# Moving the normalisation step (subtract the mean, multiply by the reciprocal root) from DVE to POOL in a two-block transformer kernel

## The chip, the cores and the metric

The kernel runs on one core of one Trainium2 chip. The metric is the device time of one execution in microseconds (us). PE is the matrix engine, DVE the vector engine, ACT the scalar engine, POOL the GpSimd engine, SP the engine that only issues DMAs here.

## The reference, cut to what matters

Two blocks run over 16 sequences of 128 tokens with 128 channels and 16 heads of 8 channels. The first is a cross attention with a conditioned layer norm on both inputs; the second is a self attention, a cross attention and an MLP.

```python
def _ada_ln(x, c, W_ss, b_ss):                 # block 0, on x and on the context
    mu = mean(x); var = mean((x - mu) ** 2)
    h = (x - mu) / sqrt(var + EPS)
    scale, bias = split(silu(c) @ W_ss + b_ss, 2)
    return (1 + scale)[:, None, :] * h + bias[:, None, :]
x = x + attention(q(ada_ln(x)), kv(ada_ln(ctx))) @ Wp + bp
...
x = x + gate_a * (self_attention(modulate(_ln(x))) @ W_proj + b_proj)      # block 1
x = x + cross_attention(_ln(x), _ln(ctx)) @ W_cproj + b_cproj
x = x + gate_m * (gelu(modulate(_ln(x)) @ W_mlp1 + b_mlp1) @ W_mlp2 + b_mlp2)
```

Each `(x - mu) * rsqrt(var + eps)` is what the change is about.

## The kernel before, in words

**Work.** There are three attention layers (CROSS0, SELF1, CROSS1), then the MLP. A unit is one sequence in one layer: 48 units, in 12 groups of 4; the MLP has 4 more groups. Every engine runs its own program, written out by hand in a loop over ticks, from -10 to 53, and semaphores tie them together. In tick t the stages of several units stand side by side: scores of unit t+2, row maxima of t+2 and t+1, the second score product (with the row maximum folded in, "keyed") of unit t, the product with the values of t and t-1, and the output projection of t-2. There is a front of work once per group, spread over the ticks 4g-10 to 4g-7: the norm of x in the first (n = 0), the norm of the context in the second (n = 1, only where the layer has one), the projections to q, k, v in the rest. So there are 24 norms: 16 of x and 8 of the context.

**A norm.** DVE makes the statistics of four sequences (`norm_stats`: L705, L708, and L710, which adds epsilon). POOL makes the reciprocal root of 128x4 values by a power (`inverse_root`, L858). DVE then subtracts the mean and multiplies by the root, four instructions of 128x128 (`normalise`, L721), at the end of its tick. PE transposes the four results one tick later in program order (`transpose_normed`, L339), ACT scales and shifts them (`modulate`, L558 or L553), PE projects them (L349, L357). In CROSS1 the context's statistics are those of CROSS0, so DVE only adds another epsilon.

**The row maximum.** PE makes the scores of a unit in two halves (`scores`, L374), and each half waits until DVE has reduced the half before (`row_max`, L740, 1.2 us). After the second half POOL splits the 128x16 maxima into two bf16 parts (`split_max`, L865 and L867), PE turns them (`turn_max`, L382), DVE copies them out of PSUM (`copy_max_rows`, L749), SP sends them by DMA into rows of `stack_q`, and then PE may start the keyed scores of that unit (`keyed_scores`, L398).

**PSUM slots.** All small products of PE share three slots of `misc_ps` in a fixed order (`MISC_ORDER`). PE may take a slot when the use three places earlier has been read out. In a tick of CROSS0 with a norm, the slot of `transpose_normed` is that of the gate product before (read by DVE in `copy_gates`, L779), and the slot of `turn_summed` (L428) is that of `turn_max` (read by `copy_max_rows`).

**Orders around the change.** The order of DVE in a tick is

```python
row_max(tick + 2, 0); copy_max_rows(tick + 1); norm_stats(*norm); leave_rest(g3, 1)
add_branch(tick - 2); divide(tick - 1); row_max(tick + 2, 1)
normalise(*norm); copy_gates(tick); leave_rest(g2, 0)
```

and that of POOL is

```python
add_gated(tick - 3)  or  add_out_bias(tick - 2)
inverse_root(*norm); split_rest(g3, 1); split_max(tick + 2); split_rest(g2, 0)
```

(each where its unit or group exists; there is a norm in the first tick of a group's front, and in the second where the layer has a context norm). PE's order in a tick is keyed scores, first half (L398); scores of t+2, first half (L374); attend t-1 (L418); `turn_max` (L382); `transpose_normed` (L339); `project_out` (L440); keyed scores, second half; `turn_summed` (L428); scores, second half; projections; attend t; `turn_attn` (L433). `divide` (L755, L759) needs L428, and its result is turned by L433.

The other names: `x_bias` (L893) is x plus the output's bias, made by POOL for `add_branch` (L773); in SELF1 POOL makes the gated addition instead (L899, L901); `split_rest` (L877, L879) splits q and k into bf16 parts, on the two ticks of a group's front that have no norm in steady running.

## Time and profile before

| What | Value |
|---|---|
| Median of 3 runs | 353.94 us (353.48 to 354.7) |
| The profiled execution's own time | 353.89 us |
| Its span in the trace | 352.1 us |
| PE busy (matmuls) | 280.2 us, 80% |
| DVE busy | 248.9 us, 71% |
| ACT busy | 206.0 us, 59% |
| POOL busy | 130.4 us, 37% |
| Chain that ended last | PE 44%, DVE 25%, issue 15%, DMA 5%, ACT 4%, POOL 3% |
| of it the line of `normalise` (L721) | 6% |

The chain that ended last is followed back from the last instruction, at each step to what released it. "Issue" in it is time in which an engine waited for nothing that the profile shows. Engines are not busy in sum: at every point one of them holds the others up, and which one has to be read in the timeline.

### The profile page before, as it was taken

The numbers are of one execution on the slowest core, as the hardware profiler recorded it, in microseconds if no ns is written. First come the engines' busy times: TensorE is split into PE (matmuls) and PEld (weight loads), VectorE is DVE, ScalarE is ACT, GpSimd is POOL, SyncE is SP. The second block draws the span as 40 slices with busy tenths as digits, with TensorE's granted clock in tenths as the row PEclk, the third lists the DMA queues.
The fourth block names the chain that finished last, engine by engine and source line by source line (L and its number), as shares of the span: only waits on it lengthen the run. The fifth ranks groups of instructions, "written<-read, shape, count | busy, mean of one in ns | idle before, by whom it ended". The sixth has DMA issues, their size and how long they took to land.

```text
span 352.1 us, 10184 instructions
## 1 busy us (share of the span) xinstructions
PE 280.2 (80%) x3827; PEld 179.9 (51%) x3827; DVE 248.9 (71%) x630; ACT 206.0 (59%) x323; POOL 130.4 (37%) x252
## 2 busy tenths in 40 slices
PE   0415346988989899898988979889798878879894
PEld 0403224655656566565565656656565555544442
DVE  7374478798787877878788797887978787713104
ACT  1004224777675676767766757667667757775540
POOL 1863362522524315252453644536443131301000
PEclk9999685999999999999999999999999999999999
DMA  8901431323123222332322323322322300000013
GB/s 230 271 0 45 135 89 48 86 56 90 53 76 80 77 72 71 85 81 68 93 73 71 93 60 83 93 63 78 90 67 78 93 6 4 4 1 2 1 30 89
DMA packets 31904, 25.39 MB, mean 72 GB/s; under 512 B 4552, under 2 KB 31600, under 8 KB 31856
## 3 DMA queue, kind: packets, MB, share of 16 engines
q1 hardware_dynamic: 30624, 23.74, 25.1%
q10 hardware_dynamic: 1232, 1.00, 1.0%
q8 instruction: 31, 0.51, 0.6%
q14 instruction: 17, 0.14, 0.1%
HBM read 4.41 MB, written 1.05 MB: 16 GB/s over the span
## 4 chain that ended last, share of the span: by engine, by line
PE 44%; DVE 25%; issue 15%; DMA 5%; ACT 4%; POOL 3%; SPq 2%; ACTq 1%; DVEq 0%; POOLq 0%
PE misc_ps L349 7%; PE attn_ps L418 7%; DVE normed L721 6%; DVE neg_max L740 4%; PE keyed_ps L398 4%; DMA stack_q<-max_rows 4%; PE score_ps L465 4%; PE keyed_ps L454 4%; PE score_ps L374 3%; DVE stats L705 3%; PE misc_ps L428 3%; PE misc_ps L357 3%; DVE rest L732 2%; PE misc_ps L333 2%; ACT parts L572 2%
## 5 line engine op out<-in xcount | busy, mean ns | idle before, releaser
L740 DVE TENSOR_REDUCE neg_max<-score_ps 128x8 f32<-128x1024 f32 x96 | 116.7, 1216 | 15.0 <-PE score_ps L374 15.0
L592 ACT ACTIVATE probs<-keyed_ps 128x1024 f32<-128x1024 f32 x96 | 98.3, 1024 | 12.9 <-PE keyed_ps L398 10.4
L418 PE MATMUL attn_ps<-probs,values 128*32 128x128 f32 x1536 | 61.8, 279 | 0.4 <-ACT probs L592 0.4
L398 PE MATMUL keyed_ps<-stack_q,stack_k 64*128 64x128 bf16 x768 | 38.6, 221 | 10.9 <-DMA stack_q<-max_rows 9.8
L418 PEld LDWEIGHTS attn_ps<-probs,values 128*32 128x32 f32 x1536 | 36.1, 109 | 19.1 <-issue 10.6
L374 PE MATMUL score_ps<-stack_k,stack_q 62*128 62x128 bf16 x768 | 38.8, 221 | 8.9 <-DVE neg_max L740 8.9
L858 POOL TENSOR_TENSOR rstd<-var_eps,minus_half 128x4 f32<-128x4 f32 x24 | 24.4, 1016 | 57.7 <-DVE var_eps L710 57.7
L865 POOL CAST max_parts<-neg_max 128x16 bf16<-128x16 f32 x48 | 10.2, 212 | 89.9 <-DVE neg_max L740 89.7
L558 ACT ACTIVATE normed_t<-misc_ps,mod 128x128 f32<-128x128 f32 x48 | 18.0, 456 | 40.5 <-PE misc_ps L339 40.5
L339 PE MATMUL misc_ps<-ident,normed 128*128 128x128 f32 x96 | 18.3, 322 | 24.9 <-DVE normed L721 22.0
L609 ACT ACTIVATE attn_t<-misc_ps,bcol 128x128 f32<-128x128 f32 x48 | 17.6, 368 | 32.3 <-PE misc_ps L433 30.8
L398 PEld LDWEIGHTS keyed_ps<-stack_q,stack_k 64*128 64x128 bf16 x768 | 21.9, 95 | 25.1 <-DMA stack_q<-max_rows 15.4
L732 DVE SCALAR_TENSOR_TENSOR rest<-misc_ps,bcol_p,parts 128x512 f32<-128x512 f32 x24 | 18.0, 751 | 23.0 <-ACT parts L572 23.0
L374 PEld LDWEIGHTS score_ps<-stack_k,stack_q 62*128 62x128 bf16 x768 | 23.7, 96 | 19.3 <-DVE neg_max L740 11.6
L428 PE MATMUL misc_ps<-ident,summed 128*128 128x128 f32 x192 | 31.1, 284 | 2.7 <-ACT summed L600 0.3
L600 ACT ACTIVATE summed<-attn_ps 128x512 f32<-128x512 f32 x48 | 28.5, 593 | 3.6 <-PE attn_ps L418 3.6
L879 POOL TENSOR_TENSOR parts<-rest,parts 128x512 bf16<-128x512 f32 x24 | 27.7, 1155 | 1.9
L349 PE MATMUL misc_ps<-normed_t,w_qk 128*128 128x512 f32 x48 | 28.2, 676 | 0.0
L339 PEld LDWEIGHTS misc_ps<-ident,normed 128*128 128x128 f32 x96 | 11.9, 159 | 29.8 <-DVE normed L721 29.7
L572 ACT ACTIVATE parts<-misc_ps,bcol_p 128x512 bf16<-128x512 f32 x24 | 16.5, 687 | 15.6 <-PE misc_ps L349 15.6
L428 PEld LDWEIGHTS misc_ps<-ident,summed 128*128 128x128 f32 x192 | 20.1, 140 | 9.9 <-ACT summed L600 4.5
L877 POOL CAST parts<-rest 128x512 bf16<-128x512 f32 x24 | 14.6, 609 | 25.9 <-DVE rest L732 25.9
(92 smaller groups left out, 411.7 us busy)
## 6 DMA issues: line engine op xcount, KB each, us to landing
stack_q<-parts SPq DMA_DIRECT2D x72, 128.0 KB, 2.4
stack_k<-parts SPq DMA_DIRECT2D x72, 128.0 KB, 2.4
stack_q<-max_rows SPq DMA_DIRECT2D x96, 4.0 KB
xs<-in_x_dram SPq DMA_DIRECT2D x4, 256.0 KB, 4.4
cs<-in_ctx_dram SPq DMA_DIRECT2D x4, 256.0 KB, 5.1
out_dram<-xs SPq DMA_DIRECT2D x4, 256.0 KB, 2.3
w<-in_L_xcond_W_mlp_dram SPq DMA_DIRECT2D x2, 256.0 KB, 5.8
wmod<-in_L_xcond_W_mod_dram ACTq DMA_DIRECT2D x1, 384.0 KB, 5.7
```

The lines of the kernel that those rows point to most:

```text
L339: mm = pe.transpose(ps[:, j * T:(j + 1) * T], normed[:, n, j, :], ident[:, :])
L349: pe.matmul(take_misc("qk"[n], g), w_qk[:, s, n, :], normed_t[:, src, :, :], start=True, stop=True).then_inc(qk_ps, 1)
L374: mm = pe.matmul(score_ps[:, e, a * T:(a + 1) * T], stack_q[rows, g % STACKS, CP * c + a, cols], stack_k[rows, g % STACKS, CP * c + a, col ...
L398: mm = pe.matmul(keyed_ps[:, e, a * T:(a + 1) * T], stack_k[rows, g % STACKS, CP * c + a, cols], stack_q[rows, g % STACKS, CP * c + a, col ...
L418: mm = pe.matmul(attn_ps[at:at + QUAD, slot * T:(slot + 1) * T], values[:, u // PER % STACKS, u % PER, h, :], probs[:, n % 3, (CP * e + a) ...
L428: mm = pe.transpose(ps[:, i * 128:(i + 1) * 128], summed[:, u % 2, i, :], ident[:, :])
L592: act.activation(probs[:, n % 3, :], keyed_ps[:, :, :].rearrange("t e n -> t (e n)"), ACT.Exp, scale=float(D) ** -0.5).then_inc(probs_read ...
L600: act.activation(summed[:, u % 2, :, :].rearrange("p s t -> p (s t)"), attn_ps[:, :], ACT.Copy).then_inc(summed_ready, 1)
L732: dve.scalar_tensor_tensor(out=rest[:, n, :], in0=misc("qk"[n], g), scalar=bcol_p[:, r:r + 1], in1=parts[:, g % 2, n, 0, :], op0=ALU.add, ...
L740: dve.tensor_reduce(neg_max[:, u % 2, :, CP * c:CP * (c + 1)], score_ps[:, :, :].rearrange("t e (a k) -> t e a k", k=T), AX.X, ALU.max, ne ...
L858: pool.tensor_tensor(rstd[:, n, :], var_eps[:, n, :], minus_half[:, :], ALU.pow).then_inc(rstd_ready, 1)
L879: pool.tensor_tensor(parts[:, g % 2, n, 2, :], rest[:, n, :], parts[:, g % 2, n, 1, :], ALU.subtract).then_inc(split_ready, 1)
```

## The change

The function `normalise` moves from DVE's program to POOL's. Its four instructions stay the same (tensor_scalar with subtract and mult, mean and root read per partition), with the same two waits, and POOL runs them straight after its reciprocal root, ahead of `split_rest(g3, 1)` and `split_max(tick + 2)`. DVE's `norm_stats` gets a new wait: before it writes the statistics of input n, the last norm of that input must have been taken (`normed_ready`), since another engine now reads them. `norm_input` moves out to where both engines see it.

```diff
+        def earlier_norm(g, n):
+
+            return max((norms_to(*m) for m in NORMS[:norms_to(g, n) - 1] if m[1] == n), default=0)
...
@@ DVE, norm_stats
+                if earlier_norm(g, n):
+
+                    dve.wait_ge(normed_ready, earlier_norm(g, n))
...
@@ DVE
-            def normalise(g, n):
-                b0, b1 = batches(g)
-                src, mv = norm_input(g, n)
-                dve.wait_ge(rstd_ready, norms_to(g, n))
-                if g >= 1:
-
-                    dve.wait_ge(normed_ps, norms_to(g, n) - 1)
-                for j in range(PER):
-                    ins = dve.tensor_scalar(normed[:, n, j, :], src[:, b0 + j, :], mv[:, j, 0:1],
-                                            rstd[:, n, j:j + 1], ALU.subtract, ALU.mult)
-                ins.then_inc(normed_ready, 1)
...
@@ DVE, loop over ticks
                 if unit(tick + 2):
                     row_max(tick + 2, 1)
-                if norm:
-                    normalise(*norm)
                 if 0 <= tick < B:
                     copy_gates(tick)
...
@@ POOL
+            def normalise(g, n):
+                b0, b1 = batches(g)
+                src, mv = norm_input(g, n)
+                pool.wait_ge(rstd_ready, norms_to(g, n))
+                if g >= 1:
+
+                    pool.wait_ge(normed_ps, norms_to(g, n) - 1)
+                for j in range(PER):
+                    ins = pool.tensor_scalar(normed[:, n, j, :], src[:, b0 + j, :], mv[:, j, 0:1],
+                                             rstd[:, n, j:j + 1], ALU.subtract, ALU.mult)
+                ins.then_inc(normed_ready, 1)
...
@@ POOL, loop over ticks
                 if norm:
                     inverse_root(*norm)
+                    normalise(*norm)
                 if g3 is not None:
                     split_rest(g3, 1)
```

POOL's instructions in CROSS1, in the two ticks of a group that hold its norms of x and of the context. Before:

```order
L893 TENSOR_TENSOR x_bias<-xs,b_out 128x128
L858 TENSOR_TENSOR rstd<-var_eps,minus_half 128x4
L865 CAST max_parts<-neg_max 128x2x8
L867 TENSOR_TENSOR max_parts<-neg_max,max_parts 128x2x8
L893 TENSOR_TENSOR x_bias<-xs,b_out 128x128
L858 TENSOR_TENSOR rstd<-var_eps,minus_half 128x4
L865 CAST max_parts<-neg_max 128x2x8
L867 TENSOR_TENSOR max_parts<-neg_max,max_parts 128x2x8
```

With the change:

```order
L898 TENSOR_TENSOR x_bias<-xs,b_out 128x128
L851 TENSOR_TENSOR rstd<-var_eps,minus_half 128x4
L861 TENSOR_SCALAR normed<-xs,x_mv,rstd 128x128 x4
L870 CAST max_parts<-neg_max 128x2x8
L872 TENSOR_TENSOR max_parts<-neg_max,max_parts 128x2x8
L898 TENSOR_TENSOR x_bias<-xs,b_out 128x128
L851 TENSOR_TENSOR rstd<-var_eps,minus_half 128x4
L861 TENSOR_SCALAR normed<-cs,c_mv,rstd 128x128 x4
```

The four subtractions stand between the root and the split of the row maximum.

DVE's instructions in SELF1, from the norm of x of a group to the next tick (L770 is the branch of SELF1 in `add_branch`). Before:

```order
L710 TENSOR_SCALAR var_eps<-x_mv 128x4
L770 TENSOR_TENSOR branch<-misc_ps,b_out 128x128
L755 RECIPROCAL r_sum<-misc_ps 128x16
L759 TENSOR_TENSOR attn<-misc_ps,r_sum 128x128
L740 TENSOR_REDUCE neg_max<-score_ps 128x2x4
L721 TENSOR_SCALAR normed<-xs,x_mv,rstd 128x128 x4
L740 TENSOR_REDUCE neg_max<-score_ps 128x2x4
L749 COPY max_rows<-misc_ps 32x128
```

With the change:

```order
L717 TENSOR_SCALAR var_eps<-x_mv 128x4
L765 TENSOR_TENSOR branch<-misc_ps,b_out 128x128
L750 RECIPROCAL r_sum<-misc_ps 128x16
L754 TENSOR_TENSOR attn<-misc_ps,r_sum 128x128
L735 TENSOR_REDUCE neg_max<-score_ps 128x2x4 x2
L744 COPY max_rows<-misc_ps 32x128
```

The two reductions, one of the second half of a unit's scores and one of the first half of the next unit's, now follow each other.

## Rows read from the trace of the kernel before

**Rows 1.** The page: busy time of each engine, and PE's granted clock in 40 slices.

```profile
PE 280.2 (80%) x3827; PEld 179.9 (51%) x3827; DVE 248.9 (71%) x630; ACT 206.0 (59%) x323; POOL 130.4 (37%) x252
...
PEclk9999685999999999999999999999999999999999
```

**Rows 2.** Groups by line and form: busy us, mean ns | idle before, releaser.

```profile
L721 DVE TENSOR_SCALAR normed<-xs,x_mv,rstd 128x128 f32<-128x128 f32 x64 | 19.8, 372 | 4.8 <-POOL rstd L858 4.8
...
L721 DVE TENSOR_SCALAR normed<-cs,c_mv,rstd 128x128 f32<-128x128 f32 x32 | 9.6, 364 | 2.3 <-POOL rstd L858 2.3
```

**Rows 3.** Groups by line and form: POOL's other operations on 128x128.

```profile
L893 POOL TENSOR_TENSOR x_bias<-xs,b_out 128x128 f32<-128x128 f32 x32 | 15.1, 472 | 2.0 <-DVE xs L773 2.0
...
L841 POOL COPY w_qk<-wq 128x128 f32<-128x128 f32 x1 | 0.4, 389 | 0.0
...
L828 POOL TENSOR_SCALAR_AFFINE_SELECT ident<-ident 128x128 f32<-128x128 f32 x1 | 0.3, 293 | 0.2 <-POOL ident L826 0.2
L831 POOL CAST ident_b<-ident 128x128 bf16<-128x128 f32 x1 | 0.3, 291 | 0.1
```

**Rows 4.** Timeline, CROSS0, a tick with norm and gate, and POOL's next split: start us, us, instruction.

```profile
118.64 1.02 POOL L858 TENSOR_TENSOR rstd<-var_eps,minus_half 128x4 f32<-128x4 f32 x1 [3.11 <-DVE var_eps L710]
...
125.72 0.20 POOL L865 CAST max_parts<-neg_max 128x16 bf16<-128x16 f32 x1 [4.26 <-DVE neg_max L740]
125.99 0.22 POOL L867 TENSOR_TENSOR max_parts<-neg_max,max_parts 128x16 bf16<-128x16 f32 x1
...
120.29 1.25 DVE L721 TENSOR_SCALAR normed<-xs,x_mv,rstd 128x128 f32<-128x128 f32 x4
...
121.22 0.22 PE L382 MATMUL misc_ps<-ident_b,max_parts 128*32 128x128 bf16 x1
122.02 0.63 PE L339 MATMUL misc_ps<-ident,normed 128*128 128x128 f32 x4 [0.58 <-DVE gate L779]
```

**Rows 5.** Timeline, CROSS1, a tick with norm but no gate, and the next.

```profile
267.79 1.02 POOL L858 TENSOR_TENSOR rstd<-var_eps,minus_half 128x4 f32<-128x4 f32 x1 [2.67 <-DVE var_eps L710]
...
271.75 0.20 DVE L749 COPY max_rows<-misc_ps 32x128 bf16<-32x128 bf16 x1
...
273.27 1.21 DVE L740 TENSOR_REDUCE neg_max<-score_ps 128x8 f32<-128x1024 f32 x1
...
270.75 0.66 PE L339 MATMUL misc_ps<-ident,normed 128*128 128x128 f32 x4 [0.15 <-DVE normed L721]
...
272.10 0.63 PE L428 MATMUL misc_ps<-ident,summed 128*128 128x128 f32 x4
...
274.56 0.40 PE L398 MATMUL keyed_ps<-stack_q,stack_k 64*128 64x128 bf16 x8 [0.66 <-DMA stack_q<-max_rows]
274.79 0.39 PE L374 MATMUL score_ps<-stack_k,stack_q 62*128 62x128 bf16 x8
```

**Rows 6.** Timeline, the start: the norms of groups 0 and 1.

```profile
22.30 1.03 POOL L858 TENSOR_TENSOR rstd<-var_eps,minus_half 128x4 f32<-128x4 f32 x1 [0.39 <-DVE var_eps L710]
...
36.14 1.01 POOL L858 TENSOR_TENSOR rstd<-var_eps,minus_half 128x4 f32<-128x4 f32 x1
...
26.99 1.11 DVE L721 TENSOR_SCALAR normed<-cs,c_mv,rstd 128x128 f32<-128x128 f32 x4 [1.13 <-POOL rstd L858]
...
40.83 1.11 DVE L721 TENSOR_SCALAR normed<-cs,c_mv,rstd 128x128 f32<-128x128 f32 x4 [1.13 <-POOL rstd L858]
```

**Rows 7.** Timeline, the context norm of group 2.

```profile
57.02 1.01 POOL L858 TENSOR_TENSOR rstd<-var_eps,minus_half 128x4 f32<-128x4 f32 x1 [2.82 <-DVE var_eps L710]
...
59.15 0.29 PE L382 MATMUL misc_ps<-ident_b,max_parts 128*32 128x128 bf16 x1
```

**Rows 8.** Timeline, the context norm of group 3, and the MLP's third norm.

```profile
82.39 0.63 PE L339 MATMUL misc_ps<-ident,normed 128*128 128x128 f32 x4 [0.58 <-DVE gate L779]
...
305.53 1.02 POOL L858 TENSOR_TENSOR rstd<-var_eps,minus_half 128x4 f32<-128x4 f32 x1 [1.84 <-DVE var_eps L710]
...
308.05 0.66 PE L339 MATMUL misc_ps<-ident,normed 128*128 128x128 f32 x4 [0.56 <-DVE normed L721]
```

More of the change, by code:

```diff
@@ L194, in norms_to, with norm_input @@
             return NORMS.index((g, n)) + 1
+        def earlier_norm(g, n):
+            return max((norms_to(*m) for m in NORMS[:norms_to(g, n) - 1] if m[1] == n), default=0)
+        def norm_input(g, n):
+            b0, b1 = batches(g)
+            return (cs, c_mv[:, b0:b1, :]) if n else (xs, x_mv)
         def stat_steps_to(g, n):
@@ L685, in _ @@
                                   ALU.add).then_inc(mod_ready, 1)
-            def norm_input(g, n):
-                b0, b1 = batches(g)
-                return (cs, c_mv[:, b0:b1, :]) if n else (xs, x_mv)
             def norm_stats(g, n):
@@ L711, in norm_stats @@
                 assert stat_steps[0] == stat_steps_to(g, n)
-            def normalise(g, n):
-                b0, b1 = batches(g)
-                src, mv = norm_input(g, n)
-                dve.wait_ge(rstd_ready, norms_to(g, n))
-                if g >= 1:
-                    dve.wait_ge(normed_ps, norms_to(g, n) - 1)
-                for j in range(PER):
-                    ins = dve.tensor_scalar(normed[:, n, j, :], src[:, b0 + j, :], mv[:, j, 0:1],
-                                            rstd[:, n, j:j + 1], ALU.subtract, ALU.mult)
-                ins.then_inc(normed_ready, 1)
             def leave_rest(g, n):
@@ L858, in inverse_root @@
                 pool.tensor_tensor(rstd[:, n, :], var_eps[:, n, :], minus_half[:, :], ALU.pow).then_inc(rstd_ready, 1)
+            def normalise(g, n):
+                b0, b1 = batches(g)
+                src, mv = norm_input(g, n)
[6 more added lines that the diff above has]
+                ins.then_inc(normed_ready, 1)
             def split_max(u):
```

## The prediction
> **What bounds the kernel now.** I read the page first. PE is busy 80%, DVE 71%, POOL only 37%, and PE's granted clock is low in three slices near the start alone (6, 8 and 5 tenths) [rows 1]. So neither PE nor DVE bounds the whole, and POOL looks idle. The groups by line give the work that moves: 64 and 32 subtractions on DVE, 19.8 + 9.6 = 29.4 us [rows 2]. The chain of waits gives L721 6% of the span, some 21 us. Neither number is the gain, and the timeline says why. It shows three kinds of tick with a norm.
>
> With a gate product (groups 3 to 6), PE turns the row maximum at 121.22 and could go on, but the transposes start only at 122.02: their PSUM slot is the gate product's, and DVE reads that out after the four subtractions, 0.58 us late by the row [rows 4]. Without a gate (groups 7 to 13), PE waits 0.15 us for the subtractions at 270.75, then 0.66 us for the DMA of the row maximum at 274.56, whose copy on DVE (271.75) stood behind the subtractions and the reduction after them [rows 5]. At the start everything is one chain: statistics, root, subtractions, transposes [rows 6]. So per norm in steady running only about 0.6 us is open to be won. That is a bound on the saving, 12 x 0.6 = 7 us, not 29.
>
> **What the change does to these waits.** DVE loses 1.25 us in each of the ticks. POOL gains the same four instructions, and what is queued behind them there is `split_max`. Who waits for that: `turn_max` on PE, and since PE runs in order, the transposes and all that follows. Before, DVE's subtractions ran beside `split_max`. Now root, subtractions, split, turn and transposes are in series. The whole answer hangs on the length b of the block of four on POOL.
>
> **The price b.** POOL runs no such tensor_scalar before, so I bound it by what POOL does on 128x128 [rows 3]. With one input: the cast 0.291 us and the affine select 0.293 us; the permuting copy 0.389 us. With two inputs: 0.472 us. In a row of equal instructions each overlaps the last by some 0.05 us (an estimate from the two copies of weights, which start 0.34 apart and take 0.39). That makes b = 4 x 0.29 - 0.15 = 1.01 us at the low end, and 4 x 0.47 - 0.15 = 1.73 us at the high end. The operation reads one tensor, which speaks for the cast, but it has two arithmetic steps and fetches two values per partition, which costs something I cannot see. I take the row in between, the copy: b = 4 x 0.39 - 0.15 = 1.41 us. Both ends stay for the range.
>
> **The sum, at b = 1.41.** The two splits with the handover between them take 125.99 + 0.22 - 125.72 = 0.49, say 0.50 us, and the handover alone, from one POOL instruction to one that waits for it, is 0.07 to 0.08 us [rows 4]. From the split to `turn_max` on PE I estimate 0.15 us, and from that to the transposes 0.17 us (what they would have followed by at 121.39 had the slot been free). So the transposes start at (end of the root) + 0.08 + b + 0.50 + 0.15 + 0.17 = end of the root + 0.90 + b.
>
> 1. Start, group 0. POOL starts the first root at 22.30 and does both norms back to back: DVE's statistics of the context no longer queue behind the first subtractions, and are ready in time. End: 22.30 + 1.03 + 0.08 + b + 1.02 + 0.08 + b = 24.51 + 2b = 27.33; before, 26.99 + 1.11 = 28.10 [rows 6]. Gain 0.77 us.
> 2. Start, group 1. Likewise from 36.14: 36.14 + 1.01 + 0.08 + b + 1.01 + 0.08 + b = 38.32 + 2b = 41.14, before 40.83 + 1.11 = 41.94 [rows 6]. Gain 0.80 us.
> 3. Group 2, context norm. `turn_max` was at 59.15; now 57.02 + 1.01 + 0.08 + b + 0.50 + 0.15 = 58.76 + b = 60.17 [rows 7]. PE then has no wait for several us that could absorb it. Loss 1.02 us; its norm of x before that, about 0.1 us more.
> 4. Groups 4, 5, 6, a norm of x in a tick with a gate. The transposes come at 118.64 + 1.02 + 0.90 + b = 120.56 + b = 121.97 instead of 122.02 [rows 4]. Gain 0.05 us each, 0.15 us.
> 5. Group 3 has two such ticks. In the second DVE had been the bound all along (its statistics make it late). It now comes in with the row maximum's copy 0.9 us earlier, and with it the second half's scores, which waited for DVE, and the transposes at 82.39, which waited for the gate [rows 8]. POOL starts this root about 0.95 us earlier, so the transposes come at some 81.4. Gain 1.0 us for both ticks together.
> 6. Groups 7 to 13, no gate. The transposes come at 268.81 + 0.90 + b = 271.12, 0.37 us later than 270.75 [rows 5]. `turn_summed` at 272.10 had 0.12 us of slack, since it waited for the copy of the row maximum, which is now early; it comes 0.25 us late, and so do `divide` and the next reduction (273.27 to 274.48, now to 274.73). The scores at 274.79 had waited behind the DMA, so these 0.25 us are covered, and the DMA's 0.66 us can't be cashed, because the scores need the reduction. Gain 0.0 us, seven times.
> 7. The second tick of groups 8 to 11: POOL's subtractions of the context are done before the row maximum is, so nothing is queued behind them that is ready; DVE's copy comes earlier and PE gets about 0.1 us. Gain 0.4 us.
> 8. The MLP's third norm ends at 305.53 + 1.02 + 0.08 + b = 308.04, and the transposes were at 308.05 [rows 8]. Loss about 0.05 us. The fourth has 10 us of room.
>
> Sum: 0.77 + 0.80 - 1.02 - 0.10 + 0.15 + 1.0 + 0 + 0.4 - 0.05 = 1.95 us. The profiled execution took 353.89 us by its own time (1.8 beside its span of 352.1), as good as the median of 353.94, so the forecast is 352.0 us.
>
> The rest costs nothing that I count. DVE's new wait in `norm_stats` is for a norm four ticks back, or one done microseconds before. POOL's `x_bias` and gated additions come up to a microsecond later, but DVE uses them after the output projection on PE, which comes no earlier. SP's queue is not touched. In the start the statistics' small add on DVE may run into POOL's block; POOL needs its result only after the block.
>
> The slope is what matters: b enters twice in items 1 and 2 and once in items 3, 4 (three times), 5, 6 (seven times) and 8, so a tenth of a microsecond more in b costs about 17 x 0.1 = 1.7 us. A whole us of gain needs b below 1.47, and above 1.59 the kernel is slower by over a us.
>
> **A rule against it.** DVE's own block takes 1.25 us in a busy tick [rows 4]; 1.41 is 13% above that. The Trainium skill says otherwise ("GPSIMD Engine Reference", section Engine selection): elementwise work belongs on VectorE, GpSimd is about twice as slow, though it calls operations with one input roughly line-rate. By its first half the block would be 2.5 us, a rival below; by its second the low end, 1.01 us. POOL's cast and its two-input add stand at 0.29 and 0.47 us [rows 3], on either side of DVE's 0.37 [rows 2], so the trace does not settle it.
>
> **Rivals.**
> - *The block as fast as the cast, b about 1.0 to 1.25.* For: the affine select does several steps per element at the cast's price. Item by item at b = 1.01: 1.57 + 1.58 - 0.62 + 3 x 0.45 + 1.4 + 7 x 0.3 + 0.4, which is 7.8 us, so 346 us; at 1.25 it is about 349.
> - *The row maximum queues behind the block (slower).* Place: POOL's `split_max`, then `turn_max` at the head of PE's queue. It decides from b = 1.59 on. At b = 1.73, as for two inputs, 17 x 0.32 = 5.4 us are lost against the forecast: 357.4 us; at 1.85 it is 359.5. For: two arithmetic steps, and two operands fetched per instruction. Against: only one tensor is read.
> - *The block is twice DVE's, b = 2.5.* Then 17 x 1.09 = 18.5 us: 370.5 us. Against: every other simple operation on 128x128 on POOL takes under 0.5 us.
> - *No change.* Gain and loss cancel, b near 1.5 to 1.6, or the slack on PE is a little less than I read: 353 to 355 us.
> A second uncertainty is the clock: it is low in slices 5 to 7 of 40, where PE has holes [rows 1], and shifts of items 1 to 3 can move that by about a us either way.
>
> **How the numbers follow.** 0.3%, 1.1 us, is about what a measurement of this kernel can tell from no change. I give my forecast's own case (350 to 352.9) 0.30, the fast block 0.16, no change 0.16, the queue behind POOL 0.29, twice DVE's price 0.09. So faster 0.46, same 0.16, slower 0.38. Cases of both signs hold most of the chance; the likeliest one's own range is 350 to 352.9, and the whole range 347 to 361 leaves out half of the fastest case and the price of twice DVE's.
>
> **What would show it.** In the profile after: the mean of the POOL rows of `normed` (0.39 expected) and the length of four; DVE busy down by 29 us and POOL up by as much or a little more; `turn_max` in norm ticks later by some 0.7 us with PE idle before it, released by POOL; the wait for the gate gone; the wait of the keyed scores for the DMA after a norm tick about halved; the norms of group 0 and 1 done 0.8 us earlier. I am wrong if the four take more than 1.6 us, or if PE's wait for `max_parts` appears and the time still falls by several us.

## The result and the profile after

The kernel got slower, by far more than I had allowed for: 398.98 us in the median (398.38 to 401.63) against 354.32 for the kernel before in the same job, a ratio of 1.1257 (95% interval 1.1220 to 1.1295). The forecast was 352.0 us, in a range of 347 to 361. The profiled execution took 399.31 us, with a span of 397.5 (before: 353.89 and 352.1), so there are 45.4 us of span to explain. One execution of one kernel below (the block behind the split, 426.15 us) ran in a slower state of the chip and is left out of its figures.

The page of the kernel after, against [rows 1]:

```profile
PE 303.0 (76%) x3827; PEld 193.1 (49%) x3827; DVE 226.5 (57%) x534; ACT 206.3 (52%) x323; POOL 202.9 (51%) x348
...
PEclk9999585796989969989898998989989696999999
...
PE 45%; POOL 29%; issue 12%; DVE 6%; ACT 4%; DMA 2%; ACTq 1%; SPq 0%; POOLq 0%; DVEq 0%
POOL normed L861 14%; PE attn_ps L427 7%; PE misc_ps L358 6%; PE misc_ps L437 5%; PE keyed_ps L407 4%; POOL rstd L851 4%; PE misc_ps L348 4%; POOL parts L884 4%; PE score_ps L383 4%; PE score_ps L474 3%; PE keyed_ps L463 3%; DVE rest L727 2%; POOL parts L882 2%; ACT parts L581 2%; PE misc_ps L449 2%
```

Three things stand in it. POOL is busy 72.5 us longer, where I expected 29 or a little more. POOL holds 29% of the chain that ended last, before it held 3%. And PE does the same 3827 matmuls in 23 us more, because its granted clock is no longer full: it falls to 5 to 8 tenths in slice after slice, and its mean is 0.90 (before 0.976 in the profiled execution, 0.962 to 0.976 in the others).

The groups by line and form give the price (busy us, mean ns), against [rows 2] and [rows 3]:

```profile
L861 POOL TENSOR_SCALAR normed<-xs,x_mv,rstd 128x128 f32<-128x128 f32 x64 | 50.0, 793 | 1.7
...
L861 POOL TENSOR_SCALAR normed<-cs,c_mv,rstd 128x128 f32<-128x128 f32 x32 | 25.0, 793 | 0.9 <-POOL rstd L851 0.2
...
L898 POOL TENSOR_TENSOR x_bias<-xs,b_out 128x128 f32<-128x128 f32 x32 | 14.5, 454 | 0.6 <-DVE xs L768 0.6
```

One subtraction takes 793 ns on POOL. That is 2.1 times DVE's 372 and 364, and 1.7 times POOL's own addition of two tensors (L898). The block of four is 3.13 us, 2.5 times DVE's 1.25.

The timeline, CROSS0, a tick of the kind of [rows 4] (there it is group 5's norm of x, here group 4's; start us, us, instruction):

```profile
111.24 1.03 POOL L851 TENSOR_TENSOR rstd<-var_eps,minus_half 128x4 f32<-128x4 f32 x1 [3.11 <-DVE var_eps L717]
...
112.37 3.13 POOL L861 TENSOR_SCALAR normed<-xs,x_mv,rstd 128x128 f32<-128x128 f32 x4
...
113.37 0.65 PE L427 MATMUL attn_ps<-probs,values 128*32 128x128 f32 x16
...
115.45 0.20 POOL L870 CAST max_parts<-neg_max 128x16 bf16<-128x16 f32 x1
115.73 0.22 POOL L872 TENSOR_TENSOR max_parts<-neg_max,max_parts 128x16 bf16<-128x16 f32 x1
...
116.00 0.23 PE L391 MATMUL misc_ps<-ident_b,max_parts 128*32 128x128 bf16 x1 [1.99 <-POOL max_parts L872]
...
116.17 0.97 PE L348 MATMUL misc_ps<-ident,normed 128*128 128x128 f32 x4
...
116.27 0.21 DVE L744 COPY max_rows<-misc_ps 32x128 bf16<-32x128 bf16 x1 [1.56 <-PE misc_ps L391]
...
120.31 0.64 PE L427 MATMUL attn_ps<-probs,values 128*32 128x128 f32 x16
```

The series is the one that the prediction named: root, block, split, turn (L391), transposes (L348). Its formula puts the transposes at end of root + 0.90 + b = 112.27 + 0.90 + 3.13 = 116.30, and they come at 116.17. The wait for the gate product is gone. In its place PE stands for 1.99 us behind POOL's split. Over the span PE's sum of this wait is 27.2 us in 13 places.

The hole has a second effect. The same four transposes take 0.97 us instead of 0.63, and from them to the second attention of the tick (L427) it is 120.31 - 116.17 = 4.14 us. Before it was 124.87 - 122.02 = 2.85 us:

```profile
124.87 0.64 PE L418 MATMUL attn_ps<-probs,values 128*32 128x128 f32 x16
```

PE's granted clock in this tick was 0.68 from 116 to 117 us, 0.50 from 117 to 119, 0.61 from 119 to 120, and 1.00 again from 120.

### The profile page after: what moved, and what is told of

Its sections match the earlier page's. It is cut to its first block, busy times and chain, and to the rows that moved or that the text cites. A ratio compares the mean times of both kernels' runs of the same rounds, so it can differ in the third digit from the quotient of the medians.

```text
span 397.5 us, 10202 instructions
## 1 busy us (share of the span) xinstructions
PE 303.0 (76%) x3827; PEld 193.1 (49%) x3827; DVE 226.5 (57%) x534; ACT 206.3 (52%) x323; POOL 202.9 (51%) x348
## 4 chain that ended last, share of the span: by engine, by line
PE 45%; POOL 29%; issue 12%; DVE 6%; ACT 4%; DMA 2%; ACTq 1%; SPq 0%; POOLq 0%; DVEq 0%
POOL normed L861 14%; PE attn_ps L427 7%; PE misc_ps L358 6%; PE misc_ps L437 5%; PE keyed_ps L407 4%; POOL rstd L851 4%; PE misc_ps L348 4%; POOL parts L884 4%; PE score_ps L383 4%; PE score_ps L474 3%; PE keyed_ps L463 3%; DVE rest L727 2%; POOL parts L882 2%; ACT parts L581 2%; PE misc_ps L449 2%
## 5 line engine op out<-in xcount | busy, mean ns | idle before, releaser
L427 PE MATMUL attn_ps<-probs,values 128*32 128x128 f32 x1536 | 66.2, 293 | 0.4 <-ACT probs L601 0.4
L861 POOL TENSOR_SCALAR normed<-xs,x_mv,rstd 128x128 f32<-128x128 f32 x64 | 50.0, 793 | 1.7
L427 PEld LDWEIGHTS attn_ps<-probs,values 128*32 128x32 f32 x1536 | 38.4, 114 | 21.8 <-issue 13.1
L383 PE MATMUL score_ps<-stack_k,stack_q 62*128 62x128 bf16 x768 | 41.7, 233 | 8.3 <-DVE neg_max L735 8.3
L851 POOL TENSOR_TENSOR rstd<-var_eps,minus_half 128x4 f32<-128x4 f32 x24 | 24.7, 1030 | 45.6 <-DVE var_eps L717 45.4
L407 PE MATMUL keyed_ps<-stack_q,stack_k 64*128 64x128 bf16 x768 | 41.0, 231 | 5.6 <-DMA stack_q<-max_rows 4.6
L348 PE MATMUL misc_ps<-ident,normed 128*128 128x128 f32 x96 | 20.7, 353 | 27.7 <-POOL normed L861 27.7
L437 PE MATMUL misc_ps<-ident,summed 128*128 128x128 f32 x192 | 36.3, 319 | 0.8 <-ACT summed L609 0.3
L383 PEld LDWEIGHTS score_ps<-stack_k,stack_q 62*128 62x128 bf16 x768 | 25.7, 101 | 20.4 <-DVE neg_max L735 10.4
L391 PE MATMUL misc_ps<-ident_b,max_parts 128*32 128x128 bf16 x48 | 11.0, 230 | 27.2 <-POOL max_parts L872 27.2
L358 PE MATMUL misc_ps<-normed_t,w_qk 128*128 128x512 f32 x48 | 29.8, 711 | 0.0
L884 POOL TENSOR_TENSOR parts<-rest,parts 128x512 bf16<-128x512 f32 x24 | 27.7, 1155 | 1.9
L348 PEld LDWEIGHTS misc_ps<-ident,normed 128*128 128x128 f32 x96 | 13.2, 174 | 30.8 <-POOL normed L861 29.1
L882 POOL CAST parts<-rest 128x512 bf16<-128x512 f32 x24 | 14.6, 609 | 25.3 <-DVE rest L727 25.3
```

The costliest lines, as they stand in the source:

```text
L348: mm = pe.transpose(ps[:, j * T:(j + 1) * T], normed[:, n, j, :], ident[:, :])
L358: pe.matmul(take_misc("qk"[n], g), w_qk[:, s, n, :], normed_t[:, src, :, :], start=True, stop=True).then_inc(qk_ps, 1)
L383: mm = pe.matmul(score_ps[:, e, a * T:(a + 1) * T], stack_q[rows, g % STACKS, CP * c + a, cols], stack_k[rows, g % STACKS, CP * c + a, col ...
L407: mm = pe.matmul(keyed_ps[:, e, a * T:(a + 1) * T], stack_k[rows, g % STACKS, CP * c + a, cols], stack_q[rows, g % STACKS, CP * c + a, col ...
L427: mm = pe.matmul(attn_ps[at:at + QUAD, slot * T:(slot + 1) * T], values[:, u // PER % STACKS, u % PER, h, :], probs[:, n % 3, (CP * e + a) ...
L437: mm = pe.transpose(ps[:, i * 128:(i + 1) * 128], summed[:, u % 2, i, :], ident[:, :])
```

## The experiments

Theory A was first that the block's length alone, times my slope of 17 us per us, gives the loss; the rival was that the place in POOL's queue or the clock gives it. Each kernel changes the one after the change, unless the text says otherwise. All times are medians, all ratios are to the kernel before in the same job.

### What one subtraction costs on POOL

A probe, one execution: the four instructions of a norm take other forms in some layers, so what it computes is no layer norm there.

```diff
+                if layer(g) == SELF1:
+                    ins = pool.tensor_scalar(normed[:, n, :, :], src[:, b0:b1, :], mv[:, 0, 0:1],
+                                             rstd[:, n, 0:1], ALU.subtract, ALU.mult)
+                elif layer(g) == LAYERS:
+                    ins = pool.tensor_tensor(normed[:, n, :, :], src[:, b0:b1, :],
+                                             mv[:, :, 0:1].broadcast_to([T, PER, H]), ALU.subtract)
...
+                    pool.tensor_scalar(normed[:, n, 1, :], src[:, b0 + 1, :], 0.01,
+                                       1.02, ALU.subtract, ALU.mult)
+                    pool.tensor_scalar(normed[:, n, 2, :], src[:, b0 + 2, :], mv[:, 2, 0:1],
+                                       None, ALU.subtract)
+                    ins = pool.tensor_scalar(normed[:, n, 3, :], src[:, b0 + 3, :], 0.01,
+                                             None, ALU.subtract)
```

> Forms of POOL's instruction, one look for their durations; the output is not the reference's. In the norms of CROSS0 and CROSS1 the four subtractions take four forms on 128x128: two values per partition and two steps; two immediates and two steps; one value per partition and one step; one immediate and one step. In SELF1 one instruction on 128x512 with two values per partition replaces the four; in the MLP's norms one tensor_tensor on 128x512 subtracts the broadcast means, and the product with the root is left out. Theory 1 (the arithmetic is slow): both two-step forms take 0.79 us, both one-step forms 0.3 to 0.55. Theory 2 (fetching the values per partition is slow): the immediates take 0.3 to 0.4 us in both forms, the others 0.5 to 0.8. The 128x512 form tells fixed from running cost: near 1.2 us if some 0.65 us of the 0.79 is fixed, near 3 us if all of it runs with the elements. The broadcast form should take 1.16 us, as the plain two-input one does.

The groups by line and form (mean ns is the second number):

```profile
L861 POOL TENSOR_SCALAR normed<-xs,x_mv,rstd 128x512 f32<-128x512 f32 x4 | 8.3, 2077 | 0.4
L867 POOL TENSOR_SCALAR normed<-cs,c_mv,rstd 128x128 f32<-128x128 f32 x8 | 6.4, 798 | 0.9 <-POOL rstd L851 0.2
...
L869 POOL TENSOR_SCALAR normed<-xs 128x128 f32<-128x128 f32 x8 | 5.1, 642 | 0.0
...
L871 POOL TENSOR_SCALAR normed<-cs,c_mv 128x128 f32<-128x128 f32 x8 | 4.8, 604 | 0.0
L873 POOL TENSOR_SCALAR normed<-cs 128x128 f32<-128x128 f32 x8 | 4.2, 527 | 0.0
...
L864 POOL TENSOR_TENSOR normed<-xs,x_mv 128x512 f32<-128x512 f32 x4 | 4.2, 1042 | 0.3
```

The barest form, one step with a constant, takes 527 ns. A value per partition instead of the constant adds 77, the second step 115, so 527 + 2 x 77 + 115 = 796, as measured (797). So neither theory of the probe holds alone: the second step and the fetched values cost 269 ns together, but two thirds of the price is there without them. All four forms of tensor_scalar cost POOL more than its two-tensor operations (454 to 472), and the barest is nearly twice its cast. Nor is it DVE's work beside it: in the kernel after, all 96 last 791 to 799 ns, those of group 1 too, during which DVE stands nearly idle (0.2 us busy between 40 and 50 us). From 128 to 512 elements it grows by (2077 - 797)/384 = 3.3 ns per element. One instruction over 512 elements is thus shorter than four over 128 (2.08 against 3.13 us), but it has one mean and one root per partition, and the four sequences have four. With the mean broadcast, one two-tensor operation does 128x512 in 1.04 us.

### The block's length: two and three of the four left out

```diff
+            pool.memset(normed[:, :, 2:PER, :], 0.5)       # 1:PER in the second kernel
...
-                for j in range(PER):
+                for j in range(2):                          # range(1)
```

> The change with only two of the four subtractions of each norm; the other two are left out and their sequences read a constant instead. The block is then b = 1.55 us instead of 3.13. Theory A (the sum of the prediction was right and only b was mis-sized): at b = 1.55 that sum gives 354.4 us. Theory B (the sum is wrong in itself, the series on POOL costs more than it says): 362 us or more.

> The change with only one of the four subtractions of each norm; three are left out and their sequences read a constant. b = 0.79 us. Theory A (the sum of the prediction): the gains are capped by what else holds PE, some 345 to 347 us. Theory B (the relief of DVE is worth little, since PE or the row maximum's loop holds the tick anyway): 351 us or more. Together with the two-subtraction kernel and the change this gives the time at b = 0.79, 1.55 and 3.13: if the slope from 1.55 to 3.13 is 17 us per us, as in the sum, the change would take 381 us; it takes 399, so a steeper part is expected, 28 us per us, and PE's granted clock should be 0.98 of full in the two short ones against 0.90 in the change.

Two of four: 356.72 us (355.76 to 358.12), ratio 1.0062 (1.0040 to 1.0084). Three of four left out: 343.39 us (342.70 to 344.57), ratio 0.9677 (0.9640 to 0.9713). The blocks are 1.58 and 0.79 us. My sum gives 352.0 + 17 x 0.17 = 354.9 for the first (1.8 less than measured) and 352.0 - 17 x 0.62 = 341.5 for the second (1.9 less). The kernel before is 354.97 us in this job, 1.0 above the 353.94 from which I had started, so 0.8 and 0.9 us of these misses are the sum's own. The slope between the two medians is 13.3/0.79 = 17 us per us, as predicted; the two profiled executions alone give 11.2/0.79 = 14, so it is known to a few us per us. The first time lies between the two theories on record (354.4, and 362 or more), nearer to A; the second lies below A's 345 to 347, so the gains had no cap there. So the terms of the sum stood as a whole, up to about 2 us. From 1.58 to 3.13 us the slope is 42.3/1.55 = 27 us per us: something else begins above.

### The block as two broadcast operations

```diff
-                for j in range(PER):
-                    ins = pool.tensor_scalar(...)
+                pool.tensor_tensor(normed[:, n, :, :], src[:, b0:b1, :],
+                                   mv[:, :, 0:1].broadcast_to([T, PER, H]), ALU.subtract)
+                pool.tensor_tensor(normed[:, n, :, :], normed[:, n, :, :],
+                                   rstd[:, n, :].unsqueeze(2).broadcast_to([T, PER, H]), ALU.mult)
```

> The change with POOL's block written as two tensor_tensor operations over 128x512, a subtraction with the mean broadcast along the channels and a product with the root broadcast, in place of four tensor_scalar operations. Nothing is left out. By the probe one such operation takes 1.04 us, so the block is 2 x 1.04 + 0.08 = 2.2 us instead of 3.13. Theory A (the length of the block sets the time, by the curve of the versions with parts left out: 356.7 us at 1.57, some 27 us per us above it): 370 to 377 us. Theory B (the form of the instructions matters too, as DVE and POOL get into each other's way in SBUF with it): over 380 us.

371.06 us (369.67 to 373.06), ratio 1.0471 (1.0442 to 1.0500), the clock's mean 0.938. The same tick as above:

```profile
102.23 1.02 POOL L852 TENSOR_TENSOR rstd<-var_eps,minus_half 128x4 f32<-128x4 f32 x1 [3.10 <-DVE var_eps L718]
103.33 1.05 POOL L861 TENSOR_TENSOR normed<-xs,x_mv 128x512 f32<-128x512 f32 x1
104.46 1.04 POOL L864 TENSOR_TENSOR normed<-normed,rstd 128x512 f32<-128x512 f32 x1
105.44 0.20 POOL L873 CAST max_parts<-neg_max 128x16 bf16<-128x16 f32 x1
```

The time lies in theory A's 370 to 377: the length counts, and the form beside it not by much. Full work in 2.2 us instead of 3.13 is worth 28 us, and still slower than before. PE's wait at the turn is 0.98 us in this tick, and the transposes take 0.66 us.

### Four or eight or fourteen products in PE's hole

PE gets extra products ahead of its wait for the split, written to columns that nobody reads, in the 18 ticks that have both a norm and a unit.

```diff
             def turn_max(u, fill=False):
-                pe.wait_ge(max_split, 2 * (u + 1))
                 ps = take_misc("max", u)
+                if fill:
+                    for i in range(14):                     # 8, 4 in the other two
+                        pe.matmul(ps[:, 256:384], ident[:, :], ident[:, :], start=True, stop=True)
+                pe.wait_ge(max_split, 2 * (u + 1))
```

> The change with 14 extra products of 128x128 on PE (some 0.9 us or more of work at full clock each time, written to columns nobody reads) in each tick with a norm, ahead of PE's wait for the split of the row maximum, so in the hole that POOL's block opens there. Nothing is left out. Theory A (part of the loss is PE's granted clock, which falls behind the hole: 0.90 on average against 0.976 before): the granted clock in the steady windows comes back to 0.95 or more, the stretch from the transposes to the next attention shortens from 4.1 us towards 2.9 us, and the time falls from 399 to 383 to 390 us. Theory B (the hole alone costs, and the low clock is only a companion): the time stays at 398 to 402 us or rises.

> The change with eight extra products of 128x128 on PE ahead of its wait for the split, in each tick with a norm that has a unit (18 of them): 1.94 us by the 0.121 us of each of the 28 passes of the fill before, in a hole of 2.0 us. Nothing is left out. Theory A (the low granted clock behind the hole costs 1.2 us per such tick): the clock comes back to 0.95 or more and the time falls to 378 to 386 us. Theory B (the hole alone costs; that the transposes to attention stretch fell from 4.1 to 2.9 us with the longer fill is offset elsewhere): 398 to 402 us.

> As the run with eight extra products, with four, 0.97 us, so that half of the hole is left. Theory A with a hole of 1 us still low enough to lose the clock at times: between the two, 386 to 396 us. If half the filling keeps the whole clock: 378 to 386 us. Theory B: 398 to 400 us.

Fourteen: 416.06 us (415.68 to 416.73), ratio 1.1740 (1.1716 to 1.1765), clock 0.964. They took 3.39 us, far more than the 0.9 I had put on record, and overfilled the hole; neither theory's number came. Eight: 393.42 us (392.39 to 394.53), ratio 1.1083 (1.1054 to 1.1112), clock 0.964, outside both ranges. Four: 391.06 us (390.05 to 391.37), ratio 1.1018 (1.0994 to 1.1041), clock 0.955. That is in theory A's 386 to 396 for a half-filled hole; the reason given for it, that the clock would be lost at times, is not what the windows below show. So PE does more work, and the kernel is 7.9 us faster with four extra products per norm tick. Here is that tick:

```profile
113.44 1.16 PE L392 MATMUL misc_ps<-ident 128*128 128x128 f32 x8
115.52 0.23 PE L394 MATMUL misc_ps<-ident_b,max_parts 128*32 128x128 bf16 x1 [0.92 <-POOL max_parts L875]
115.68 0.66 PE L348 MATMUL misc_ps<-ident,normed 128*128 128x128 f32 x4
...
118.56 0.65 PE L430 MATMUL attn_ps<-probs,values 128*32 128x128 f32 x16
```

The transposes take 0.66 us again, and from them to the attention it is 2.88 us, not 4.14: 1.26 us per such tick went with the granted clock behind the hole. The windows of 25 us, after the change and then with four products (busy us of PE, PEld, DVE, ACT, POOL; granted clock; DMA share; GB/s):

```profile
100.00:125.00 25.00, 22.46 (x313) 14.76 (x312) 16.99 (x40) 14.96 (x24) 10.91 (x21) 0.93 0.25 67
125.00:150.00 25.00, 22.46 (x310) 14.64 (x308) 16.03 (x38) 14.64 (x23) 10.91 (x21) 0.86 0.25 65
```

```profile
100.00:125.00 25.00, 23.40 (x352) 15.59 (x353) 17.68 (x42) 15.82 (x25) 11.36 (x23) 1.00 0.26 69
125.00:150.00 25.00, 23.40 (x349) 15.61 (x344) 18.37 (x41) 16.29 (x26) 11.81 (x23) 1.00 0.29 76
```

The starts of the roots on POOL give the loss by stage, from one profiled execution each. I take the first root of the groups 4, 8 and 12:

| Span, us | before | after | four products | eight | after - before | four - before | eight - before |
|---|---|---|---|---|---|---|---|
| to group 4 | 96.63 | 111.24 | 110.74 | 109.80 | 14.6 | 14.1 | 13.2 |
| groups 4 to 7 | 85.95 | 98.21 | 92.23 | 92.24 | 12.3 | 6.3 | 6.3 |
| groups 8 to 11 | 85.21 | 94.86 | 95.63 | 101.00 | 9.7 | 10.4 | 15.8 |
| 12 to the end | 84.31 | 93.19 | 90.40 | 89.46 | 8.9 | 6.1 | 5.1 |

With the clock full, groups 4 to 7 lose 6.3/4 = 1.57 us each. My items 4 and 6 give 3.13 - 1.46 = 1.67 and 1.72. In these four groups the low clock costs 6.0 us more, and after group 12, where eight products keep the granted clock at 1.00 in both windows from 300 to 350 us, 3.7 us more. The table also shows why eight products missed both ranges: they are as good as four or better everywhere but in groups 8 to 11. There the second tick of a group leaves PE a shorter hole: the products end at 213.5 us, about 1 us after the split is done, so they delay what they were to shield.

In groups 8 to 11 the filling gains nothing, and the timeline of the kernel after shows what holds there:

```profile
209.45 1.03 POOL L851 TENSOR_TENSOR rstd<-var_eps,minus_half 128x4 f32<-128x4 f32 x1 [2.13 <-DVE var_eps L717]
...
210.58 3.13 POOL L861 TENSOR_SCALAR normed<-xs,x_mv,rstd 128x128 f32<-128x128 f32 x4
...
214.12 0.45 POOL L904 TENSOR_TENSOR branch<-branch,gate 128x128 f32<-128x128 f32 x1
...
214.65 0.45 POOL L906 TENSOR_TENSOR xs<-xs,branch 128x128 f32<-128x128 f32 x1
...
215.06 1.03 POOL L851 TENSOR_TENSOR rstd<-var_eps,minus_half 128x4 f32<-128x4 f32 x1
...
216.19 3.13 POOL L861 TENSOR_SCALAR normed<-cs,c_mv,rstd 128x128 f32<-128x128 f32 x4
...
219.27 0.20 POOL L870 CAST max_parts<-neg_max 128x16 bf16<-128x16 f32 x1
```

These groups have two norms in two neighbouring ticks, and POOL runs through both without a pause, 10.3 us from 209.45 to the second split. From root to root it is 5.61 us (before 182.58 to 186.90, 4.32), and from the second root to the next group's 18.13 (before 16.98): each of the two ticks is longer, by 1.29 and 1.15 us, where my items had 1.72 in the first and a gain of 0.1 in the second. PE's clock is low there too (0.77 from 216 to 222 us), but with four products and a clock of 1.00 the same two distances are 5.64 and 18.27 us, no shorter: the slow work on PE lies beside POOL's queue.

### The block behind the split

```diff
                 if norm:
                     inverse_root(*norm)
-                    normalise(*norm)
...
                     split_max(tick + 2)
+                if norm:
+                    normalise(*norm)
```

> POOL makes the four subtractions behind the split of the row maximum instead of ahead of it; nothing else differs from the change. Theory A (the queue): the time is lost because the split of the row maximum stands behind 3.13 us of subtractions. Then turn_max comes on time again and the kernel returns to 354 to 362 us. Theory B (the series): PE runs in order and has to have the four results at its transposes wherever the split stands. The root's end plus the split's 0.5 us plus 3.13 us is later than now, so PE waits some 2.5 us at the transposes instead of 2 us at turn_max, and the time is 398 us or up to 406 us.

422.56 us (418.31 to 423.99 in five executions), ratio 1.1905 (1.1862 to 1.1949), worse than the change and beyond the 398 to 406 of theory B. The waits:

```profile
PE misc_ps L348 <- POOL normed L861: 73.8, 23, 11.6
```

The row maximum is turned in time, but the transposes stand right behind the turn in PE's order, and PE waits 73.8 us for them in 23 places (with the change 27.7 in 5 places, and 27.2 for the split). So B's mechanism is what came, with a size that it had too small. Whichever stands first on POOL, PE needs both.

### Transposes later in the tick

In PE's, ACT's and the PSUM slots' orders the transposes and the scaling move behind the second half of the scores. First in the kernel **before**, then with the change and POOL's block behind the split.

```diff
-                    + [("norm", g1, 0)] * (g1 is not None) + [("norm", g2, 1)] * ...
                     + [("k", g3)] ... + [("proj", tick - 2)] ... + [("out", tick - 1)] ...
+                    + [("norm", g1, 0)] * (g1 is not None) + [("norm", g2, 1)] * ...
```

> The kernel before with PE's transposes of the norm moved behind the second half of the scores in the same tick, the order of the PSUM slots and ACT's scaling moved with them; the subtractions stay on DVE. Theory A (what was open to be won lies in PE's in-order wait at the transposes, 0.58 us with a gate, 0.15 without): the wait goes and the kernel is faster by 1 to 5 us. Theory B (PE is bound by the loop of the row maximum and its DMA, so its work has only changed places): within 1 us of before.

> The change with all four subtractions on POOL, but behind the split of the row maximum, and with PE's transposes behind the second half of the scores. Theory A (the loss in steady running is PE's wait in the series root, block, transposes, plus the low granted clock behind it): PE reaches the transposes about 1.6 us later and the block is 3.13 us, so the wait per norm tick falls from 2 us to about 0.5, the clock stays at full, and only the start keeps its loss of about 5 us plus group 2: 356 to 364 us. Theory B (POOL's load or the relief of DVE has another cost of its own): 375 us or more.

In the kernel before it makes no difference: 354.28 us (353.59 to 355.75), ratio 0.9992 (0.9977 to 1.0007). With the change: 375.23 us (374.12 to 376.38), ratio 1.0585 (1.0563 to 1.0606), with the clock's mean at 0.967. That is 24 us better than the change, but not in theory A's 356 to 364; it is at the edge of theory B's 375 or more, by which POOL's load has another cost of its own. The timeline shows it:

```profile
107.61 3.14 POOL L862 TENSOR_SCALAR normed<-xs,x_mv,rstd 128x128 f32<-128x128 f32 x4
110.71 0.46 POOL L899 TENSOR_TENSOR x_bias<-xs,b_out 128x128 f32<-128x128 f32 x1
...
110.80 0.66 PE L349 MATMUL misc_ps<-ident,normed 128*128 128x128 f32 x4 [1.01 <-POOL normed L862]
111.27 0.29 DVE L769 TENSOR_TENSOR xs<-misc_ps,x_bias 128x128 f32<-128x128 f32 x1 [2.37 <-POOL x_bias L899]
```

`x_bias` is queued behind the block, and DVE waits 2.37 us for it with its reductions behind; over the span this wait is 23.9 us in 10 places, and the kernel after has none of it. PE still waits for the block too, 1.01 us here and 44.2 us in 23 places, so the two costs aren't told apart. In neither of the two places tried are 3.1 us free in POOL's queue.

### The work shared between DVE and POOL

```diff
+                for j in range(PER - 1):                    # DVE, where it was before
+                    ins = dve.tensor_scalar(...)
+                ins.then_inc(normed_dve, 1)
...
-                for j in range(PER):
+                for j in range(PER - 1, PER):               # POOL; PER - 2 with two
```

> The work is shared: DVE makes three subtractions of each norm where it made four before, POOL makes one behind its root, ahead of the split of the row maximum. Nothing is left out. POOL's block is 0.79 us, DVE's 0.9. Theory A (what costs is POOL's block in front of the split, and what helps is a shorter block on DVE): the split is ready before PE reaches turn_max, DVE is 0.3 us earlier, and the kernel is faster than before by 1 to 5 us. Theory B (any sharing costs, because PE now waits for two engines and DVE's and POOL's instructions hold each other up): same as before or up to 3 us slower.

> As the run with one, but two subtractions on each engine; nothing is left out. POOL's block is 1.57 us as in the kernel with two left out (356.7 us), DVE's 0.65. Theory A: the series on POOL sets the time, so it is within 1 us of 356.7 whatever DVE does beside it. Theory B (DVE's part costs as well): 358 us or more.

> One subtraction on POOL ahead of the split, three on DVE, as in the version that took 349.4 us, with the transposes and the scaling on ACT later in the tick. Nothing is left out. Theory A (what remains in a tick with a norm is the chain scores, reductions, row maximum, in which the transposes have no part; moving them in the kernel before made no difference): 348.5 to 350.5 us. Theory B (the transposes still wait for POOL and DVE at times, and lateness frees that): 344 to 347 us.

> Two subtractions on POOL behind the split of the row maximum, two on DVE where they were before, and the transposes and the scaling on ACT later in the tick. Nothing is left out. Theory A (what cost in the version with all four behind the split was POOL's block, that delayed x plus bias for DVE's next branch by 2.4 us; with half a block, 1.6 us, this delay goes): 348 to 353 us. Theory B (every 0.8 us of POOL's block is worth its 17 us per us wherever it stands, as half a block ahead of the split gave 358.8): 356 to 360 us.

> One subtraction on POOL behind the split of the row maximum, three on DVE, transposes and scaling later in the tick. Nothing is left out. With two and two this took 347.7 us. Theory A (both blocks are hidden there, and what counts is DVE's load before its reductions): one more subtraction on DVE, 0.37 us in each of 24 norms, of which the steady ones cost their share: 348.5 to 350 us. Theory B (POOL's 1.6 us still costs by delaying x plus bias): 345 to 347 us.

| Kernel | us | range of runs | ratio (interval) |
|---|---|---|---|
| one on POOL, ahead of the split | 349.44 | 348.95 to 350.16 | 0.9849 (0.9832 to 0.9866) |
| two on POOL, ahead of the split | 358.78 | 358.04 to 359.05 | 1.0107 (1.0092 to 1.0122) |
| one, transposes later | 348.70 | 348.40 to 349.41 | 0.9841 (0.9820 to 0.9862) |
| two, behind the split, transposes later | 347.66 | 346.90 to 348.33 | 0.9807 (0.9785 to 0.9829) |
| one, behind the split, transposes later | 348.51 | 348.16 to 350.00 | 0.9828 (0.9804 to 0.9851) |

All five do the whole work, and four of them beat both kernels. The exception has a block of 1.6 us ahead of the split, as long as that of the kernel with two left out (356.72). It costs 2 us more than that one, as theory B had it (358 or more): DVE has its two to do as well. One ahead of the split gained 5.3 us, just beyond theory A's 1 to 5. With one on POOL, moving the transposes is worth 0.7 us, within theory A's 348.5 to 350.5; one behind the split is at A's lower edge too. Two behind the split came out 0.3 us below A's range, and far from B's 356 to 360: behind the split, with the transposes later, the block of two costs 11 us less than ahead of it. Two things were changed at once there; with one on POOL the later transposes alone were worth 0.7 us. DVE's wait for `x_bias`, 23.9 us with four behind the split, is 7.4 us with two. The best, 347.66 us, in the tick of the first norm of group 9:

```profile
203.09 0.59 DVE L731 TENSOR_SCALAR normed<-xs,x_mv,rstd 128x128 f32<-128x128 f32 x2
203.24 0.24 POOL L888 CAST max_parts<-neg_max 128x16 bf16<-128x16 f32 x1 [0.78 <-DVE neg_max L750]
203.57 0.22 POOL L890 TENSOR_TENSOR max_parts<-neg_max,max_parts 128x16 bf16<-128x16 f32 x1
203.77 1.58 POOL L879 TENSOR_SCALAR normed<-xs,x_mv,rstd 128x128 f32<-128x128 f32 x2
```

The split comes when the row maximum does, and the block of 1.58 us ends (205.35) as DVE's branch, which POOL needs next, is ready (205.28). Its lead over the versions with one subtraction (347.66 against 348.51 and 348.70) is too small beside the scatter of the runs for a cause to be named.

## Why the prediction was wrong

**The step that failed is the price b.** I took 1.41 us, "the row in between, the copy", with ends of 1.01 and 1.73. It is 3.13 us, beyond both ends. I bounded it by the cast, the affine select, the copy and the two-input add because all read 128x128 on POOL, and argued from how many tensors each reads. The probe shows that this measure does not order POOL's operations: the barest tensor_scalar, with one tensor, costs 527 ns, above the two-input add. Rows of other forms of instruction were no bound for this one, and they gave no upper end.

**The rival "twice DVE's" came nearest, and I gave it 0.09.** Against it I wrote that every other simple operation took under 0.5 us. It named b = 2.5 and 370.5 us; the block is 2.5 times DVE's 1.25, not twice, and the time is 28 us above it. The Trainium skill ("GPSIMD Engine Reference", section Engine selection) says that GpSimd is about twice as slow on elementwise work with two inputs and roughly line-rate with one. This instruction reads one tensor, so it falls under the second half (that the first is for two inputs, the prediction had left out), which the trace does not bear out: 793 against DVE's 372 ns is 2.1, the size of the first. Its running cost of 3.3 ns per element is even above the 1042/512 = 2.0 of the broadcast two-input operation, launch included.

**The mechanism of the slower rival was right,** its size not. The split queues behind the block, PE waits at `turn_max`, and the transposes follow. The formula for them was 0.13 us off at a b more than twice the one it was made for.

**The second step that failed is the slope.** It held up to 1.6 us and broke above, while the slower rivals used 17 us per us up to b = 2.5. At b = 3.13 my sum gives 352.0 + 17 x 1.72 = 381.2 us, so 27.3 us of the 45.4 were in it. The other 18 by stage, from the table (5.7, 5.5, 3.2 and 3.7 us):
- The granted clock, a term that I had only as "a us either way" in the start. In the tick shown, the hole of 2 us on PE is followed by some 4 us at a lower clock. The best filled kernel in each stage is shorter than the one after the change by 1.4, 6.0 and 3.7 us, in groups 8 to 11 not at all. So at least 11 us went with the clock. It fills the whole excess in groups 4 to 7 (6.3 us lost with the clock full, 6.7 by my items) and after group 12 (5.1 lost, 5.2 by my items).
- Item 7, "nothing is queued behind them that is ready". True at 1.41 perhaps, not at 3.13: the context's block holds up the split too. My items give groups 8 to 11 4 x 1.72 - 0.4 = 6.5 us, and they lost 9.7.
- The start. Items 1, 2, 3 and 5 give 6 x 1.72 - 1.45 = 8.9 us up to group 4, and it lost 14.6. Group 1's norms end 0.3 us from the formula (44.55 + 3.12 = 47.67, against 38.94 + 2.18 + 6.26 = 47.38 from the root at 38.94). The largest single piece lies between group 2's context norm and group 3's first, 84.64 - 64.44 = 20.20 us against 16.01 before. Groups 2 and 3 have a block in two neighbouring ticks, and I counted it once in each; but the granted clock is low there too, 0.64 between 50 and 75 us (before 0.80), and eight products won back only 1.4 us up to group 4. The rest stays open.

**What hit.** The gate wait disappeared, DVE's load fell (by 22.4 us, not 29; where the rest is I did not follow), DVE's waits show none for the subtractions, so the new wait in `norm_stats` costs nothing. Of the signs named in advance, "I am wrong if the four take more than 1.6 us" is the one that came. The wait of the keyed scores for the DMA fell from 9.8 to 4.6 us, about the half that was expected, though of another kernel than the one forecast.

## What to carry to other kernels

Before moving an operation to an engine that has not run that form, time that form: here neighbours of the same shape did not bound it, and a single instruction in a probe would have decided the case. An engine that is 37% busy can still hold up a tick. What counts is which short, urgent operation stands behind the long one in its queue. A split of the work (here one or two of four) can bring a gain that the whole move loses. A slope worked out near one point holds only while the same waits are the ones that end last: here the loss grew steeper above it, with a second tick held up and a lower clock on the engine that now waits.

## What the runs showed of the hardware

- POOL's tensor_scalar on 128x128 f32: 527 ns with one constant and one step, 604 with one value per partition, 642 with two constants and two steps, 797 with two values and two steps; 2077 on 128x512 (all in the probe). Its cast takes 289 ns and its affine select 293 on the same tile.
- A two-tensor operation on 128x512 with the second operand broadcast takes 1.04 us there. Two of these (2.2 us) do what four tensor_scalars do in 3.13.
- Behind PE's holes of 2 us, one per norm tick in otherwise dense work, the granted clock of windows of 25 us was 0.86 to 0.93; with holes of 0.9 us it was 1.00. Four useless products per tick, eight f32 passes in 1.16 us, made the kernel 7.9 us faster. Of the clock's two levels, 1.2 and 2.4 GHz, the window from 117 to 119 us is at the lower (0.50); the slow transposes just before it (0.97 against 0.63 to 0.66 us, clock 0.68 from 116 to 117) mix both.
- In the fourteen-product kernel, whose clock was full there, the products of 128x128 in f32 appear as 28 passes in 3.39 us, two to a product and 0.121 us each.
